# A graph kernel's counting stage: compare constants in PSUM, three accumulation units of two banks, one more kept pair in sixteen

## The reference, cut to what matters

```python
feat = (h @ W).reshape(N, H, D)                        # 4 heads of 64
e = leaky_relu(el[src] + er[dst], 0.2)                 # a score for each edge and head
ex = exp(e - emax[dst]);  alpha = ex / segment_sum(ex, dst)[dst]
rst = segment_sum(feat[src] * alpha, dst)              # the attention layer
...
h = z @ W;  z = segment_sum(h[row] * norm, col) + b    # a graph convolution
```

## Time and profile before

| what | value |
|---|---|
| median of 3 runs | 5549.77 us (5548.1 to 5549.91) |
| the profiled execution's own time | 5546.5 us |
| its span, first to last instruction | 5544.7 us |
| granted TensorE clock, mean over the span | 0.903 |
| busy: PE / DVE / ACT / POOL | 79% / 59% / 54% / 40% of the span |
| kept gathers, first to last start | 242.38 to 1281.05 us |
| fill, first compare to last zeroing | about 278 to 1273 us |
| live gathers, first to last start | 1286.59 to 2472.00 us |

### The profile page before, as it was taken

How to read it: one execution, slowest core, us unless ns; L and a number is a source line. 1 busy time by engine, 2 the same in 40 slices (tenths; PEclk the granted TensorE clock), 3 DMA queues, 4 the chain that set the end, 5 groups by cost and what they waited for, 6 DMA issues and landing times. The chain is left out here.

```text
span 5544.7 us, 113554 instructions
## 1 busy us (share of the span) xinstructions
PE 4371.8 (79%) x23328; PEld 3443.7 (62%) x23329; DVE 3273.1 (59%) x10456; ACT 2971.1 (54%) x7576; POOL 2199.0 (40%) x2057
## 2 busy tenths in 40 slices
PE   2566655556888888874899699998999962899997
PEld 1444332224666666654799477776777752799996
DVE  7699866667999999987455523336233355222222
ACT  0325666666777777776233356665566655233332
POOL 2477777777777777763222000000000006122221
PEclk9799877668999999995899899999999975999998
DMA  4368888888888888874566266762444454566665
GB/s 134 113 206 261 276 282 286 291 289 258 236 236 237 235 235 236 235 206 136 168 180 181 62 215 223 224 217 81 137 133 134 133 154 136 172 183 183 181 180 164
DMA packets 623736, 1084.57 MB, mean 196 GB/s; under 512 B 74390, under 2 KB 502093, under 8 KB 616748
## 3 DMA queue, kind: packets, MB, share of 16 engines
q1 hardware_dynamic: 504252, 733.75, 43.1%
q0 software_dynamic: 112144, 268.88, 18.3%
q10 hardware_dynamic: 7200, 80.28, 3.6%
HBM read 782.21 MB, written 309.57 MB: 197 GB/s over the span
## 5 line engine op out<-in xcount | busy, mean ns | idle before, releaser
L755 POOL DMA_INDIRECT arena<-table,arena x1664 | 1717.4, 1032 | 515.7 <-issue 448.4
L1431 PE MATMUL banks<-parts,a_wide 128*128 128x512 f32 x4900 | 1179.8, 399 | 18.8 <-ACT a_wide L1454 18.8
L1431 PEld LDWEIGHTS banks<-parts,a_wide 128*128 128x128 f32 x4900 | 918.1, 189 | 263.8 <-ACT a_wide L1454 47.9
L955 PE MATMUL banks<-arena 128*128 128x261 f32 x3328 | 939.1, 406 | 0.0
L1454 ACT CAST a_wide<-arena 128x896 fp32r<-128x896 f16 x700 | 659.0, 942 | 422.7 <-PE banks L1431 406.9
L2176 POOL DMA_INDIRECT expert_in<-arena,slot x147 | 161.8, 1101 | 1649.9 <-DVEq L2121 1608.1
L2359 ACT ACTIVATE rings<-banks,b_sb 128x128 f32<-128x128 f32 x1296 | 369.4, 368 | 828.4 <-PE banks L2392 828.4
L2255 POOL DMA_INDIRECT x_kept<-rings,idx_ring x162 | 251.3, 1552 | 976.9 <-DMA x_kept<-rings,idx_ring 869.5
L701 PE MATMUL banks<-arena 128*128 128x392 bf16 x1480 | 384.3, 409 | 316.0 <-ACT banks L729 175.9
L2392 PEld LDWEIGHTS banks<-yt_ring,arena 128*128 128x128 f32 x5184 | 608.1, 193 | 15.4 <-DVE yt_ring L2281 4.1
L2392 PE MATMUL banks<-yt_ring,arena 128*128 128x128 f32 x5184 | 609.4, 276 | 6.1 <-DMA arena<-in_L_ffn_w 2.1
(11 more groups left out here) (370 smaller groups left out, 5824.1 us busy)
## 6 DMA issues: line engine op xcount, KB each, us to landing
arena<-counts SPq DMA_DIRECT2D x700, 224.0 KB, 2.5
arena<-in_L_ffn_W SPq DMA_DIRECT2D x114, 1024.0 KB, 9.5
edge_rows<-arena SPq DMA_DIRECT2D x364, 264.0 KB, 3.3
arena<-edge_rows SPq DMA_DIRECT2D x364, 264.0 KB
counts<-arena ACTq DMA_DIRECT2D x50, 1568.0 KB, 6.5
arena<-in_L_ffn_w SPq DMA_DIRECT2D x64, 1024.0 KB, 8.7
arena<-near_rows SPq DMA_DIRECT2D x416, 128.0 KB
expert_in<-rings SPq DMA_DIRECT2D x25, 2028.0 KB
```

What stands on the lines that cost most here:

```text
L755: pool.indirect_dma_start(out=got[:, r, j, :], out_offset=None, in_=table0, in_offset=bass.IndirectOffsetOnAxis(ap=src_sb[:, 2 * pair + j: ...
L955: last = pe.matmul(banks_a[u][:, 0:mw], onehot[:, u % GS, j, :], msg[:, u % RB, j, 0:mw], start=False, stop=False, skip_group_check=True)
L1431: last = pe.matmul(psum[u][:, 0:2 * D], a_wide[:, at:at + P], parts[:, a * 2 * D:(a + 1) * 2 * D], start=(a == 0), stop=(a == NT - 1))
```

## The change

Three things are altered together.

- The constants `lanes16` and `keys16` are moved to PSUM banks 0 and 1, as 16-bit numbers. They are made in SBUF at the end of the cooking and copied into the banks with two copies of 32-bit words. `lanes16` was made in the prologue before.
- The fill's windows rotate over the other six banks (`CB` = 6), in three units of two banks (`UW` = 2, `UR` = 3, 400 units), and TensorE's groups are of two steps (`PG` = 2). Since six is no power of two, `ptab` is now computed as the window number modulo 6, with a multiplication and a shift for the division. The cooking's transposes rotate over six banks too.
- `KEPT` has eight of 16 pairs, (0, 2, 4, 7, 9, 11, 13, 15), where it had seven, (0, 2, 5, 7, 9, 12, 14). So 832 gathers fall in the fill and 832 in the walk.

```diff
-KEPT = (0, 2, 5, 7, 9, 12, 14)
+KEPT = (0, 2, 4, 7, 9, 11, 13, 15)
-UW = 4
+UW = 2
-UR = 8 // UW
+CB = 6
+UR = CB // UW
-PG = 4
+PG = 2
...
-            lanes16 = tmp(P * LB // 2).bitcast(F16).rearrange("p (n u) -> p n u", u=LB)
+            lanes16 = psum[0].bitcast(F16).rearrange("p (n u) -> p n u", u=LB)
+            keys16 = psum[1][:, 0:KB * KEYS // 2].bitcast(F16).rearrange("p (n u) -> p n u", u=KB)
...
-                    link(dve.tensor_copy(lanes16, iota_n[:, :].unsqueeze(2).broadcast_to([P, P, LB])))
...
-                    link(dve.tensor_scalar(ptab, ptab, 7, 9, ALU.bitwise_and, ALU.logical_shift_left))
+                    turns = trow[:, 0:BP].bitcast(I32)
+                    assert CB == 6 and NW * 2731 < 1 << 24 and all(w * 2731 >> 14 == w // 6 for w in range(NW))
+                    link(dve.tensor_scalar(turns, ptab, 2731, None, ALU.mult))
+                    link(dve.tensor_scalar(turns, turns, 14, None, ALU.arith_shift_right))
+                    link(dve.scalar_tensor_tensor(out=ptab, in0=turns, scalar=-float(CB), in1=ptab,
+                                                  op0=ALU.mult, op1=ALU.add))
+                    link(dve.tensor_scalar(ptab, ptab, 8.0 - CB, 512.0, ALU.add, ALU.mult))
...
-                    link(dve.tensor_copy(keys16, kiota.unsqueeze(2).broadcast_to([P, KEYS, KB])))
+                    link(dve.tensor_copy(made_keys.bitcast(F16).rearrange("p (n u) -> p n u", u=KB),
+                                         kiota.unsqueeze(2).broadcast_to([P, KEYS, KB])))
+                    link(dve.tensor_copy(made_lanes.bitcast(F16).rearrange("p (n u) -> p n u", u=LB),
+                                         iota_n[:, :].unsqueeze(2).broadcast_to([P, P, LB])))
+                    link(dve.tensor_copy(psum[1][:, 0:KB * KEYS // 2], made_keys))
+                    link(dve.tensor_copy(psum[0][:, 0:P * LB // 2], made_lanes))
...
                 def unit(u):
-                    r = u % UR
-                    return by_bank[:, UW * r:UW * (r + 1), 0:KEYS]
+                    lo = 8 - CB + UW * (u % UR)
+                    return by_bank[:, lo:lo + UW, 0:KEYS]
```

More of the change, by code:

```diff
@@ L102 @@
 assert NVB * VB == NBP * EB and NVB <= P
-assert KEYS <= 512 and BP % OR == 0 and UW >= PG and UNITS % UR == 0
+assert KEYS <= 512 and BP % OR == 0 and UW >= PG and UR * UW == CB
 assert NG * TB == NT
@@ L444, in count_plan @@
             blank = rings[:, BCOL:BCOL + KEYS // 2].bitcast(BF16)
-            keys16 = rings[:, BCOL + KEYS // 2:BCOL + KEYS // 2 + KB * KEYS // 2].bitcast(F16).rearrange(
-                "p (n u) -> p n u", u=KB)
-            assert BCOL + (KB + 1) * KEYS // 2 <= TB * (D + AW)
+            made_keys = rings[:, BCOL + KEYS // 2:BCOL + KEYS // 2 + KB * KEYS // 2]
+            lanes_at = BCOL + (KB + 1) * KEYS // 2
+            made_lanes = rings[:, lanes_at:lanes_at + P * LB // 2]
+            assert lanes_at + P * LB // 2 <= TB * (D + AW)
             def by_pair(a):
@@ L638, in cook_dve @@
                         dve.wait_ge(pe_, 1 + n)
-                        dve.tensor_scalar((kcols16, bcols16)[a][:, k * P:(k + 1) * P], psum[n % 8][:, 0:P], 16384.0, None,
+                        dve.tensor_scalar((kcols16, bcols16)[a][:, k * P:(k + 1) * P], psum[8 - CB + n % CB][:, 0:P], 16384.0, None,
                                           ALU.min).then_inc(t_, 1)
@@ L645, in cook_pe @@
                         k, a = n // 2, n % 2
-                        if n >= 8:
-                            pe.wait_ge(t_, n - 7)
-                        pe.transpose(psum[n % 8][:, 0:P], by_pair((srcf, bf)[a])[:, k, :],
+                        if n >= CB:
+                            pe.wait_ge(t_, n - CB + 1)
+                        pe.transpose(psum[8 - CB + n % CB][:, 0:P], by_pair((srcf, bf)[a])[:, k, :],
                                      ident[:, :]).then_inc(pe_, 1)
@@ L688, in fill_pe @@
                             if p % 16 == 0:
-                                at_ = load_many(mybir.EngineType.PE, ptab, p, 16, 0, 7 * 512 + UNITS,
+                                at_ = load_many(mybir.EngineType.PE, ptab, p, 16, (8 - CB) * 512, 7 * 512 + UNITS,
                                                 "a bank masked to 7 << 9, in a leading step with a count of 1 to UNITS under it")
```

## The result

The changed kernel takes 5497.60 us (median of 4 runs, 5495.11 to 5502.16) against 5549.84 for the kernel before beside it: a ratio of 0.9909, 95% interval [0.9898, 0.9921]. That is 52 us less; the forecast was 5476, 74 less. The range of 5440 to 5600 holds it, but that range also holds no change and the slower rival at 5592; the forecast's own range, 5443 to 5529, holds it too. The profiled spans are 5493.2 and 5544.7 us, 51.5 apart. Of experiment 7's four runs one was slow, 5941.87 us at a granted clock of 0.73, and the time given there is the median of the other three. In the new file the lines have moved: gathers are line 768, compares 686 and 689, the fill's matmul 714, its eviction 737 and zeroing 742, the walk's messages 905.

What follows compares the result with a forecast made beforehand. GpSimd's gather pace was taken to bound fill and walk. The gathers' +22.9 us (prologue's 7.8 contained) and the walk's -96.8 sum to -73.9, so 5549.8 becomes 5476 us; range 5440 to 5600.

Steps and rivals of the forecast that it cites:

- the forecast's own range: Total time from 5443 to 5529 us, from the walk's 1.27 to 1.35 us a pair and the fill's 0 to +20.
- The bound: Fill and walk: GpSimd's gathers set the pace at 1.25 us each, 99% of the walk's 1100 us window.
- The hold: Fill: compares with two SBUF inputs delay gathers 79 ns each, 116.4 us together; taken as 0 after the change.
- the hold stays: Slower rival in the fill: kept gathers remain held and end 116.4 us later, total 5592 us; chance 0.14.
- The compares: Fill: with one 16-bit input in PSUM, a set of five still takes 2.53 us, the lower end.
- one element a cycle: Rival in the fill: compares from PSUM take 4.65 us a set, total 5842 us; chance 0.14.
- The prologue and the constants: Before the fill: longer table chain +7.8 us (5 to 9); constants at the cooking's end +1.5 (0 to 3).
- The gathers and the walk's start: Fill: 832 kept gathers at 1.25 us end at 1305.2, +22.9 us against 1282.3.
- The wait for the last stores: Between the last kept gather and the first live one: the idling of 4.59 us stays.
- the allowance of up to 25 us for crowded transfers: Fill: transfers meeting above 308 GB/s might delay the gathers by 0 to +25 us.
- The walk: Walk: VectorE late next at 1.27 us a pair, with 3% added 1.31, so -96.8 us (-130 to -47).
- The units: Sparse fill: three units hide latency behind ScalarE, 550 us; fill ends near 1115 us, worth nothing by itself.

Runs made afterwards that it cites:

- experiment 7: Changed kernel with two steps' banks packed in one word, so a 16-word load serves 32 steps: 5494.51 us, ratio 0.9914 to the kernel before.
- experiment 3: Kernel before with only the new eight kept pairs: 5600.99 us, ratio 1.0102 to the kernel before.
- experiment 1: Changed kernel with the compares reading their constants from SBUF copies instead of PSUM: 5613.26 us, ratio 1.0123 to the kernel before.
- experiment 5: Changed kernel with all sixteen pairs kept, so the walk has no gathers beside it; run once: 6528.27 us.
- experiment 4: Changed kernel with 32 instead of 16 words in each of TensorE's table loads: 5492.96 us, ratio 0.9906 to the kernel before.
- experiment 2: Changed kernel with the old seven kept pairs: 5548.95 us, ratio 1.0007 to the kernel before.
- experiment 9: Changed kernel with seven kept pairs, two steps' banks packed per word and 32 packed words a load: 5474.64 us, ratio 0.9873 to the kernel before.
- experiment 6: Changed kernel with two turns of the walk in each pass of its loop: 5626.89 us, ratio 1.0152 to the kernel before.
- experiment 10: Changed kernel with a hint that the loop's back edge is the likely way: 5516.31 us, ratio 0.9948 to the kernel before.

## Why the prediction was right, and where it was not

*The bound.* Right. GpSimd's pace was read as its duration plus the 0.30 us that the profile shows as idle, and the walk moved when GpSimd had one pair in sixteen less to fetch (experiment 3, at 1.326 us a pair, by that edit alone).

*The hold.* Right, in place and size: 79 ns for each compare, 116.4 us forecast, 117.1 by experiment 1. The reason taken from the walk, where a full VectorE with one input in PSUM does no harm, was the deciding one, and the rival "the hold stays" (5592) is what experiment 1 built: 5613.

The Trainium skill bears on this too: "SBUF — State Buffer", section "Who interferes with whom", says that VectorE with two SBUF inputs contends with a GpSimd instruction that reads SBUF, and that with at most one, outside the modes that use both ports of VectorE, it does not. The gathers here read their row numbers from SBUF. Experiment 1 agrees, 1247 ns beside two and 949 beside one; the price is this case's.

*The compares.* Right: the lower end was taken, 2.53 us a set, and a set now is 4 x 556 + 686 ns by its instructions' durations, less what they overlap. In VectorE's timeline of the dense fill the sets start 2.50 us apart:

```profile
285.19 0.69 DVE L686 TENSOR_TENSOR arena<-banks,arena 128x1024 bf16<-128x1024 f16 x1
...
287.69 0.68 DVE L686 TENSOR_TENSOR arena<-banks,arena 128x1024 bf16<-128x1024 f16 x1
```

The rival of one element a cycle (5842) is out.

Of the two places of the Trainium skill weighed in the prediction, "VectorE: DVE Perf Modes", section "Why PSUM operands drop a tier", is borne out at 556 ns for 784 elements; the row for a two-input instruction in "The perf-mode tier table" is not, for 16-bit numbers.

*The prologue and the constants.* Right in kind, smaller in size: +7.8 forecast, the first kept gather starts 4.5 later. The added passes were priced well, as VectorE's timeline of the table shows:

```profile
131.27 1.38 DVE L526 TENSOR_SCALAR arena<-arena 1x2368 int32<-1x2368 int32 x1
132.68 1.38 DVE L527 TENSOR_SCALAR arena<-arena 1x2368 int32<-1x2368 int32 x1
134.10 2.61 DVE L528 SCALAR_TENSOR_TENSOR arena<-arena 1x2368 int32<-1x2368 int32 x1
136.75 1.38 DVE L530 TENSOR_SCALAR arena<-arena 1x2368 int32<-1x2368 int32 x1
138.16 1.38 DVE L532 CUSTOM_DVE_ANT_0 arena<-arena 1x2368 uint16<-1x2368 uint16 x1
```

The last row started at 132.42 before, so the chain grew by 5.7 us to there. The doubling of its other steps had been charged at 2.0, and the addition, the last row, grew by only 0.19 (from 1.19). Where between the table and the first gather 1.2 us were won back was not followed.

*The gathers and the walk's start.* Right, with some luck: +22.9 forecast, +24.4 measured at the first message. The gathers' end itself moved by 20.8 (1282.3 to 1303.1), and the first message came 3.6 later behind it. The wait for the last stores, which was said to stay, did not come. The fill's own pace was as forecast too (1056 us for 832 gathers, against 1040 + 15), and the allowance of up to 25 us for crowded transfers was not needed.

*The walk.* This is the mis-sized term, and nearly the whole of the miss: -96.8 forecast, -77.0 measured. The mechanism was right, GpSimd steps back and VectorE is late next, but VectorE's floor was taken from three pairs in the middle of a turn, 1.27 us, with 3% on top for waiting. The floor is 1.33: experiment 5 has it with no gathers at all. The number stood in the prediction's own rows: VectorE's 1030.28 us of busy time in 1100 us over the 1100 / 1.426 = 771 pairs of that window make 1.336 a pair. With that floor the walk's term is (1.336 - 1.426) x 832 = -75, the sum -52, and the time 5498. That this fits to 1 us is partly luck: the same count gives 890.35 / (900 / 1.330) = 1.316 in the changed kernel and 1.307 in experiment 5, with 1 to 1.5% of idle time on top.

*The units.* Wrong, without cost here. The sparse fill was to end at 1115 by ScalarE's 3.44 us for four windows; it ended at 1288. The step that failed is that only ScalarE was counted there: TensorE stops to load its table every 16 steps, 325 us in all, and three units of two windows do not hide that. Experiments 4 and 7 took 33 and 89 us off the fill by changing the loads alone; of the rest, up to 1115, the cause is open. What I called room for compares and constants was 15 us instead of 190. With seven pairs kept this would have been the bound (experiment 2). So the change's gain is a balance: the walk's 77 us against 24 of later start, with the gathers' end only just behind the fill's.

*The rest.* The time behind the walk's end differs by 51.5 - 52.6, about 1 us.

## What to carry to other kernels

A floor for an engine that will become the bound is busy time over units of work in a whole stage (here 1.31 to 1.34 us, for 1.33), not the pace of a few good units (1.27): those leave out the price of the loop's turn. When a stall goes, look for what ends just behind it; with seven pairs kept, the fill's own end took the whole gain of the constants (experiment 2). If VectorE slows GpSimd's gathers down, look whether its instructions read two inputs from SBUF; here a constant 16-bit operand moved to PSUM freed the gathers at no cost to VectorE, for two of the eight banks. And before pricing a load by a difference of totals, look whether the trace has its rows.

## What the runs showed of the hardware that was not expected

- A table load into TensorE's registers is dear where TensorE is on the path. Sixteen words took 1.10 us at the shortest and 1.70 in the median, 32 words 2.14 to 2.37 and 2.75 to 3.08, so fewer loads of more words gained little and fewer words gained much (experiments 4, 7, 9). Why single loads take over 4 us is not settled.
- A loop body twice as long was fetched again in each pass, 212 instruction packets in 900 us instead of 5, and the walk took 5.0 us more a pass (experiment 6).
- A turn of the walk's loop costs VectorE about 0.8 us even with the single body, and the hint on its back edge added 0.4 (experiments 5, 10).
